# Experts, recurrent layer and feed-forward layer as one program over blocks of 512 tokens

## The reference

```
alpha = exp(-8 softplus(lambda) * sigmoid(x W_gate + b_gate))
beta  = sqrt(1 - alpha^2 + 1e-6)
h[t]  = alpha[t] h[t-1] + beta[t] * sigmoid(x W_in + b_in)[t] * x[t]
```

## Time and profile before

| | us |
|---|---|
| median of 3 runs | 1887.69 (1885.84 to 1889.42) |
| the profiled execution | 1888.36 |
| its span | 1886.3 |

### The profile page before, as it was taken

How to read it: one execution, slowest core, us unless ns; L and a number is a source line. 1 busy time by engine, 2 the same in 40 slices (tenths; PEclk the granted TensorE clock), 3 DMA queues, 4 the chain that set the end, 5 groups by cost and what they waited for, 6 DMA issues and landing times. The chain is left out here.

```text
span 1886.3 us, 38115 instructions
## 1 busy us (share of the span) xinstructions
PE 1624.6 (86%) x14452; PEld 1323.9 (70%) x14452; DVE 1261.5 (67%) x2637; ACT 984.7 (52%) x1929; POOL 332.3 (18%) x765
## 2 busy tenths in 40 slices
PE   3679998999999999999999999999489999772697
PEld 1457777777777777777777877877468778651486
DVE  3846676776776777777777777777455454478445
ACT  2436665665665666666666666666343222272432
POOL 3411111121111212111211211110100000073311
PEclk9879999999999999999999999999789999975699
DMA  7000000000000000000000000000121000010000
GB/s 221 1 1 2 2 2 1 2 2 2 2 2 2 2 2 1 1 2 2 2 2 2 2 2 1 2 2 2 37 64 30 1 1 1 1 54 0 1 12 34
DMA packets 23252, 23.52 MB, mean 12 GB/s; under 512 B 9356, under 2 KB 20492, under 8 KB 22948
## 3 DMA queue, kind: packets, MB, share of 16 engines
q1 hardware_dynamic: 17764, 14.77, 2.7%
q10 hardware_dynamic: 5312, 6.33, 1.2%
HBM read 19.00 MB, written 2.10 MB: 11 GB/s over the span
## 5 line engine op out<-in xcount | busy, mean ns | idle before, releaser
L711 ACT ACTIVATE pT_hi<-pT 128x512 f16<-128x512 f32 (+3 forms) x640 | 340.6, 532 | 367.5 <-PE pT L629 364.3
L832 DVE TENSOR_TENSOR pT_lo<-pT,pT_hi 128x512 f16<-128x512 f32 (+3 forms) x640 | 388.1, 607 | 158.9 <-ACT pT_hi L711 153.7
L820 DVE TENSOR_REDUCE cmx<-pS 128x1 f32<-128x512 f32 x576 | 347.8, 617 | 98.1 <-PE pS L616 94.3
L700 ACT ACTIVATE pr<-pS,nmx 128x512 f32<-128x512 f32 (+3 forms) x640 | 398.4, 623 | 11.1 <-DVE nmx L823 10.0
L629 PE MATMUL pT<-ident,pr 128*128 128x128 f32 x2176 | 346.2, 275 | 9.8 <-DVE pT_lo L832 6.3
L611 PE MATMUL pS<-lT_hi,qT_hi 128*128 128x512 f32 (+2 forms) x640 | 284.7, 445 | 57.8 <-ACT pr L700 48.4
L629 PEld LDWEIGHTS pT<-ident,pr 128*128 128x128 f32 x2176 | 258.2, 140 | 43.8 <-ACT pr L700 10.1
L671 PE MATMUL pO<-c_hi,pT_hi 128*128 128x65 f16 x2176 | 265.8, 194 | 1.2 <-DVE O L850 0.6
L672 PE MATMUL pO<-c_lo,pT_hi 128*128 128x65 f16 x2176 | 266.6, 193 | 0.0
L673 PE MATMUL pO<-c_hi,pT_lo 128*128 128x65 f16 x2176 | 263.7, 192 | 0.0
L616 PE MATMUL pS<-lT_hi,qT_lo 128*128 128x512 f32 (+2 forms) x640 | 257.3, 402 | 0.0
(11 more groups left out here) (270 smaller groups left out, 2914.8 us busy)
## 6 DMA issues: line engine op xcount, KB each, us to landing
X<-in_x SPq DMA_DIRECT2D x4, 512.0 KB, 6.9
wo<-in_w_o ACTq DMA_DIRECT2D x1, 2048.0 KB, 14.3
out<-X SPq DMA_DIRECT2D x4, 512.0 KB, 2.6
raw<-in_wd SPq DMA_DIRECT2D x14, 128.0 KB, 2.1
raw<-in_wg SPq DMA_DIRECT2D x13, 128.0 KB, 2.7
raw<-in_wu SPq DMA_DIRECT2D x13, 128.0 KB, 2.7
wqn<-in_w_qn ACTq DMA_DIRECT2D x1, 1536.0 KB, 17.9
intg<-in_qg SPq DMA_DIRECT2D x1, 768.0 KB, 5.5
```

The source lines that it names most:

```text
L700: act.activation(pr[:, at % RING, 0:n * P], pS[at % 4][:, 0:n * P], ACT.Exp, bias=nmx[:, p % 4:p % 4 + 1]).then_inc(sem("exped"), 1)
L711: act.activation(pT_hi[:, a % 4, 0:chunk[a][2] * P], src, ACT.Copy).then_inc(sem("t_hi"), 1)
L820: ch.inc(dve.tensor_reduce(cmx[:, p % 2, c:c + 1], pS[at % 4][:, 0:n * P], AX.X, ALU.max))
L832: dve.tensor_tensor(pT_lo[:, a % 4, 0:w], src, pT_hi[:, a % 4, 0:w], ALU.subtract).then_inc(sem("t_lo"), 1)
```

## The change

Router stage: stays as it is, but the constants of the recurrent layer (`lb`, `lam`, the chain of small DVE steps from `lambda` to `z`) are loaded and computed in it. SP issues two more DMAs ahead of the router's weights; one small exp is put on ACT ahead of the pieces; 16 small steps on DVE stand ahead of its wait for the logits.

All that follows is one stage with no barrier inside. Its 80 steps are the 56 expert steps and then the 24 feed-forward steps. A list of half steps (`slots`) gives the order for all engines; each engine takes from it the entries that it has a function for.

```diff
+            steps = [("moe", tb, m) for tb in range(NB) for m in range(NFM)] + [("ffn", tb, m) for tb in range(NB) for m in range(NFQ)]
...
+            for s in range(N):
+                if s + 2 < N:
+                    at_slot(2 * s, "up", s + 2)
+                if s + 1 < N:
+                    at_slot(2 * s, "split", s + 1)
+                at_slot(2 * s + 1, "down", s)
+                if s + 2 < N:
+                    at_slot(2 * s + 1, "gate", s + 2)
+
+            def add_steps(start, a):
+
+                for j in range(2):
+                    at_slot(start + j, "y_measure", (a, j))
+                    at_slot(start + 2 + j, "y_norm", (a, j))
+                    at_slot(start + 3 + j, "x_add", (a, j))
+
+            def norm_steps(start, a):
+                for j in range(2):
+                    at_slot(start + j, "x_measure", (a, j))
+                    at_slot(start + 2 + j, "x_norm", (a, j))
+                    at_slot(start + 4 + j, "x_turn", (a, j))
+
+            for tb in range(NB):
+                L0 = 2 * last_of[tb] + 1
+                at_slot(L0, "sums", tb)
+                add_steps(L0 + 1, ("moe", tb))
+                norm_steps(L0 + 5, ("moe", tb))
+                for k, (w, e) in enumerate(((1, 0), (1, 1), (0, 0), (0, 1))):
+                    at_slot(L0 + 11 + k, "lru_gate", (tb, w, e))
+                at_slot(L0 + 15, "alpha", tb)
+                at_slot(L0 + 15, "gated_x", tb)
+                at_slot(L0 + 16, "square", tb)
+                at_slot(L0 + 17, "one_less", tb)
+                at_slot(L0 + 18, "beta", tb)
+                at_slot(L0 + 19, "driven", tb)
+                for e in range(KD):
+                    at_slot(L0 + 20 + e, "scan", (tb, e))
+                for j in range(2):
+                    at_slot(L0 + 22 + j, "s_turn", (tb, j))
+                add_steps(L0 + 23, ("lru", tb))
+                norm_steps(L0 + 27, ("lru", tb))
...
+            for m in range(NFQ):
+                at_slot(2 * (NMOE - NFM + m) + 2, "pieces", ("q", m))
```

```diff
+                        for g, name in ((0, "g_up"), (1, "u_up")):
+                            bank = 2 * s + g
+                            if bank >= 3:
+                                pe.wait_ge(sem("silued" if (bank - 3) % 2 == 0 else "hidden"), (bank - 3) // 2 + 1)
...
+                        if is_routed(s):
+                            if n_routed(s) > 1:
+                                pe.wait_ge(sem("h_routed"), n_routed(s) - 1)
+                            pe.matmul(pW[0:r, :], selb[:, m * P:m * P + r], wT[:, ts], start=True, stop=True).then_inc(sem("w_up"), 1)
```

The feed-forward weights now lie in the expert weights' places (`W_all`, a slab for each piece) and take them over during the last expert block, in its steps 1 to 6, three pieces of 128 x 256 each. On DVE and ACT such a piece is:

```diff
+                            less = dve.tensor_scalar(fl[:, k % 2], rawi, -ZERO_POINT, None, ALU.add)
+                            if k % 3 == 2:
                                 ch.inc(less)
                                 ch.wait()
+                                dve.wait_ge(sem("scales_in"), 48)
+                                less = dve.tensor_tensor(fl[:, k % 2], fl[:, k % 2], sdb[:], ALU.mult)
                             less.then_inc(sem("w_float"), 1)
...
+                            dve.wait_ge(sem("w_hi"), n + 1)
```

PE waits for the turned norm of a block with its first gate and with the first feed-forward step of that block:

```diff
+                        if kind == "ffn" and m == 0:
+                            ready = ("x_turn", (("lru", tb), 1))
+                            pe.wait_ge(sem("t_hi"), hi_read[ready])
+                            pe.wait_ge(sem("t_lo"), lo_read[ready])
```

More of the change, by code:

```diff
@@ L910, in turned_norm @@
[L910 to L968, removed]
@@ L1280, in build @@
-                phase_end()
-            gated_ffn(xT, wg_, wu_, wd_, NFM, [P] * 13 + [FM - 13 * P], n_routed=FR // P, selb=selb, wT=wT,
-                      pieces=expert_pieces[3 * AHEAD:] + [(l_in, wi_[0][:], wi_[1][:]), (l_gate, wr_[0][:], wr_[1][:])],
-                      due=lambda n: range(3 * n, 3 * n + 3) if n < NFM - AHEAD else
-                      range(3 * (NFM - AHEAD) + n - NFM, 3 * (NFM - AHEAD) + n - NFM + 1) if NFM <= n < NFM + 2 else ())
-        weights.close()
-        qg_ = [sbr(weights, f"qg_{k}", [P, KD, NFQ * P], F32R) for k in range(2)]
@@ L1373, in _ @@
[L1373 to L1381 removed]
+                            mm.then_inc(sem(name), 1)
@@ new lines, in s_turn @@
+                    def s_turn(a):
+                        tb, j = a
+                        o = bank_t(("s_turn", a))
+                        pe.wait_ge(sem("scanned"), KD * (tb + 1))
+                        for q in range(2):
+                            for e in range(KD):
+                                mm = pe.transpose(o[:, (2 * q + e) * P:(2 * q + e + 1) * P], xs[:, e, (2 * j + q) * P:(2 * j + q + 1) * P], ident[:])
+                        mm.then_inc(sem("t_turned"), 1)
+                    does = {"up": up, "down": down, "x_turn": x_turn, "lru_gate": lru_gate, "s_turn": s_turn}
@@ new lines, in _ @@
+                    does = {"gate": hidden, "split": low, "y_measure": y_measure, "x_add": x_add, "x_measure": x_measure, "x_turn": x_turn,
+                            "gated_x": gated_x, "one_less": one_less, "driven": driven, "scan": scan, "pieces": pieces}
+                    for what, a in plan:
+                        if what in does:
+                            does[what](a)
+                @block.sync
+                def _(sp):
+                    sp.dma_start(sdb[:], sd.partition_broadcast(P)).then_inc(sem("scales_in"), 16)
+                    sp.dma_start(scg[:], sg).then_inc(sem("scales_in"), 16)
+                    sp.dma_start(scu[:], su).then_inc(sem("scales_in"), 16)
+                    for n, piece in enumerate(all_pieces):
+                        if n >= SLOTS:
+                            sp.wait_ge(sem("w_lo"), n - SLOTS + 1)
+                        dst = slot_of(raw, piece, n)
+                        sp.dma_start(dst.bitcast(I32) if whole_number(n) else dst, piece[0]).then_inc(sem(f"w_in{n % SLOTS}"), 16)
+                    for tb in range(NB):
+                        for j in range(2):
+                            sp.wait_ge(sem("x_added"), x_added["x_add", (("ffn", tb), j)])
+                            t = TPB * tb + 2 * j
+                            sp.dma_start(out[:, t:t + 2, :], X[:, t:t + 2, :]).then_inc(sem("dma_out"), 16)
+                    sp.wait_ge(sem("dma_out"), 16 * NB * 2)
```

935 lines of the change are left out of this document (500 added, 435 removed).

## The result

The changed kernel takes 1805.33 us, median of 4 runs (1803.56 to 1809.09), beside 1887.06 for the kernel before on the same chip: ratio 0.9568, 95% interval 0.9550 to 0.9587. The prediction was 1804 with a range of 1790 to 1830. The profiled execution took 1806.03 at a span of 1804.3.

The account below looks back on a forecast made before the run. Experts and feed-forward were taken as TensorE-bound, the 132.1 us between as bound by DVE and short chains. Stage 397.5 + 11 + 1.4 + 2 = 412; 1377.8 + 2.8 + 412 + 9.9 = 1802.5 span, giving 1804 us, range 1790 to 1830.

Parts of the forecast that it names:

- The PE stream, 397.5 us: New stage: experts 260.9, feed-forward 102.8, gates 21.8 and transposes 12.0 us of TensorE work, if nothing else delays PE.
- The pieces, 11 us: Last expert block: converting feed-forward weights, three pieces in each of six steps, leaves PE idle 11 us (9 to 14).
- DVE's loop: DVE's work and waits in a step with pieces: 7.0 us plus extras, 48.8 over six steps; PE wants 34.8.
- the slack: Routed expert step: products may come 2.8 us late before PE, wanting W's bank, has to wait.
- Last turn of x, 1.4: Before feed-forward block 3: PE waits 1.4 us for ACT's copy and DVE's low after the last recurrent block's second transposes.
- Smaller waits, 2: Across four blocks with four queues in fixed order: PE waits 0 to 8 us, taken as 2.
- rival S: New stage: short PE stalls drop the clock to its lower level, making the kernel slower, about 1934 us; chance 0.03.
- Router, +2.8: Router stage: two DMA issues and 16 small DVE steps ahead of the logits add 2.8 us (1 to 4).
- Behind the last sums, 9.9: Kernel's end: measure, root, norm and add in two halves instead of four tiles take 9.9 us (9 to 12).
- A: Pieces' steps: DVE and ACT overlap better than their order suggests, PE bound throughout, 1791 us; chance 0.12.
- E: Gates in every block: silu queues behind tanh waiting for PE's gate, uncovered table loads cost 20.5 us, 1825; chance 0.23.
- F: New stage: half the hiding fails, DVE's lateness carries into later blocks and pieces cost double, 1847 us; chance 0.04.

Follow-up runs that it names:

- e2: Changed kernel with DVE subtracting for the next piece of feed-forward weights before making the low part of the one before: 1799.37 us, ratio 0.9527.
- e1: Changed kernel without loading and converting the feed-forward weights: 1789.13 us, ratio 0.9477.
- e11: Changed kernel with the six groups of pieces one half step later, behind silu and the product of their expert step: 1804.48 us, ratio 0.9565.
- e13: e12 with the sixth and last group of pieces eight half steps later, behind alpha, beta and scan: 1793.06 us, ratio 0.9509.
- e12: Changed kernel with the edits of e2 and e11, and the last recurrent block's turning back of x one half step earlier: 1795.40 us, ratio 0.9518.
- a0: The changed kernel run again, unchanged, as the measure for its neighbours: 1806.88 us, ratio 0.9567.
- e5: Changed kernel with the norm, gates and scan chains of blocks 0 to 2 run alone, no expert step beside them: 1902.58 us, ratio 1.0080.

## Why the prediction came out right

**The PE stream, 397.5 us: right.** Without the conversion the stage is 399.9 us long, and PE is busy for 396.7 of it. Blocks 1 and 2 are 73.20 us long; the prediction said 73. Gates were 1.38 against 1.36.

**The pieces, 11 us: right in size, half right in mechanism.** The prediction gave six steps of DVE's loop as 48.8 us; the profile has 1653.29 - 1605.42 = 47.9. Three pieces took 3.9, the very sum; the subtraction of integers 0.29 for the 0.27 taken. Idle PE in the stretch is 11.0. Overlapping them alone returned 6.5 us of stage (e2), leaving them out 15.8 (e1), and moving them past silu 2.6 (e11): in four of the six steps DVE's round was the bound, as written; in the last two ACT's wait for the gates was part of it. What was wrong is what PE would be seen waiting for. I named `h_lo` or the products; it was silu in 12.1 of 14.3 us, which stands behind ACT's share of the pieces. The working had the bank that silu frees ("U of step s+3 waits for silu(s+2)") and silu's lateness ("wait for silu 0.3"), but priced the slack for W alone. Not all of the 11 us are the loop's either: 9.0 of them lie within the six steps. The last wait, 1.92 (2.36 before the load at 1658.62), comes behind alpha's table load, exp and the load back; in blocks 0 to 2 the same chain costs nothing. Taking one group of pieces from in front of it removed this wait (e13), so the pieces had used up the slack there. So the match with 11 is partly luck: the same six steps took 35.7 us in block 2 (1532.29 to 1567.99), and the loop's excess of 12.2 was 9.0 of waits and 3.1 of slower matmuls (PE busy 38.8 for 35.7), a term that the sum lacked, while the seventh step added a wait that belongs to ACT's loads as much as to the loop.

**Last turn of x, 1.4: right.** 1.5 was measured, and it went when the step was moved (e12).

**Smaller waits, 2: right.** 1.8 beside feed-forward block 0 and 0.3 for `lT_lo`, the latter inside the stretch of the pieces.

**What the sum lacked: slower matmuls behind waits.** PE is busy for 401.0 us, not 397.5 (and for 396.7 without the pieces). The chain through the pieces' stretch has groups of six that should show 1.40:

```profile
1627.33 1.67 PE pGU L1221 x6
...
1658.62 2.71 PE pGU L1221 x6
...
1663.71 1.39 PE pGU L1221 x6
```

Busy time and clock around two of the waits, of 2.36 and of 4.14 us, behind one of 0.87, and behind the first, of 2.45:

```profile
1658.60:1661.30 2.70, 2.68 (x7) 1.65 (x7) 1.90 (x3) 2.08 (x4) 0.00 (x0) 0.55 0.00 0
...
1620.40:1623.50 3.10, 3.10 (x9) 1.76 (x10) 2.96 (x8) 1.60 (x3) 0.54 (x1) 0.65 0.26 78
...
1627.30:1629.00 1.70, 1.68 (x7) 1.13 (x7) 1.38 (x2) 1.13 (x3) 0.00 (x0) 1.00 0.30 86
...
1611.70:1616.00 4.30, 4.30 (x23) 3.40 (x24) 4.20 (x8) 2.03 (x4) 0.00 (x0) 1.00 0.17 48
```

Two things are mixed. After the waits of 2.36 and 4.14 us the granted clock is at or near its lower level (0.55, 0.65) and back at 1.00 some 5 us later: rival S in small. After those of 2.45 and 2.94 us (1611.69 and 1635.68) it stays at 1.00, so the length of the wait alone doesn't decide it. The second profile of this kernel, a0, has the first of these waits, as long as here, at 1610.32, and there the clock falls behind it:

```profile
1610.00:1615.00 5.00, 4.68 (x17) 3.21 (x18) 4.80 (x11) 2.36 (x5) 0.00 (x0) 0.66 0.18 52
```

No run here shows what else decides. And a group behind a wait of only 0.87 shows 1.67 at a clock of 1.00, so 0.2 to 0.3 us belong to any restart. Within the stage the same matmuls are busy for 5.0 us less when the pieces are gone (a0 against e1). It fitted inside the range, since the stage came out at 415.3 for 412.

**Router, +2.8: in its bounds, not resolved.** The copy of the logits starts at 1361.66 us, 1.74 after its place in the earlier trace rows, and the first G at 1379.42 for 1377.78. But the first G's place varies by 3.9 us between profiles of kernels that don't differ ahead of it.

**Behind the last sums, 9.9: right.** 1794.7 to 1804.3 are 9.6.

The sum had 1802.5 for a span of 1804.3: +3.3 of stage, -1.2 at the router, -0.3 at the end. So the match within 1.3 us is partly luck: the stage came out longer by the slower matmuls, and the router's term shorter. Both are small beside the gain of 82 us. The gain itself comes from the cover, which e5 shows by taking it away (1902.6).

**The rivals.** A (no loss at the pieces) falls by e1 and the waits. E (loads break the cover in every block) falls twice: tanh needs no load of its own, 17 in all, and even with 20 more the time is 1814, not 1825. Its order of queues, silu behind a tanh that waits for PE's gate, is in the chain of the last two steps with pieces and nowhere costs PE time without them. F falls with the 152.70 of 152.70 us busy. S holds for single groups, not for the stage: the clock is 0.95 in the stretch of the pieces and 0.98 to 1.00 in the others shown.

## What to carry to other kernels

A serial chain of norms and scans that leaves TensorE idle can lie beside matmul steps at nearly no cost if it is priced engine by engine and step by step: here 79 of 132 us had no PE work, and the new stage has 14 of waiting. Price a step that several engines pass to and fro as a round (silu, products, pieces, low part, next silu), not as busy time: shortening the round by 1 us gave 3.3 to 4.0 us over four steps, moving work to an idle engine made it longer, and changing its place in the round gave almost nothing. Before moving work into emptier steps, look at what they hold already, table loads above all. And before a few microseconds are put down to an edit, compare TensorE's busy time: the same matmuls differed by up to 3.5 us between neighbours here, by where the clock fell.

## What the runs showed of the hardware

- Tanh and silu ran with no table load between them (16 tanh, 17 loads, none at tanh's line), while sigmoid asked for 12 loads of its own and 8 more to go back to silu. Exp behind tanh did load.
- POOL took 0.85 us for subtracting from 128x256 integers and 0.72 for a product of 128x256; DVE took 0.29 and 0.42.
- DVE's scan of 512 took 1.28 us where a quarter of the 2048-wide one is 1.11.
- Behind a wait of PE of 2.36 us the clock was 0.55, with six matmuls at 2.71 us in place of 1.40; behind waits of 2.45 and 2.94 in the same profile it stayed at 1.00. A restart at full clock cost 0.2 to 0.3 us.
